# Rope of the second tile half a step sooner, row units between the last transposes, and the first band tile's copies reordered

## The reference

```
x = x + band_attention(layernorm(x), ctx, ctx)     # keys within 128 rows; one head of 512; others weigh exp(-1e9)
y = layernorm(x)                                    # stream of the two layers
for l in (0, 1):
    q, k, v = split(shift_token(y) @ wqkv[l])       # 8 heads of 64
    q, k = l2norm(q) * q_scale, l2norm(k) * k_scale
    q, k = rotary with xpos scale (q, k)            # "rope"
    y = y + local_attention(q, k, v) @ wo[l]        # 256 rows back
    y = y + gated_gelu_ffn(layernorm(shift_token(y)))
x = x + y
```

## Time and profile before

| | us |
|---|---|
| median of 3 runs | 2882.83 (2881.66 to 2883.5) |
| profiled execution, its own time | 2882.62 |
| its span, first to last instruction | 2880.8 |
| PE busy | 2863.6 |
| DVE busy | 2069.0 |
| ACT busy | 1346.0 |
| POOL busy | 1308.8 |

### The profile page before, as it was taken

The page is one execution under the profiler, slowest core; times in us unless marked ns, Lnnn a source line. Parts: engine busy times, 40 slices in busy tenths (PEclk is TensorE's granted clock), DMA queues, the critical chain, the costliest instruction groups (busy, mean ns, idle before and its releaser), DMA issues. The chain is left out here.

```text
span 2880.8 us, 53016 instructions
## 1 busy us (share of the span) xinstructions
PE 2863.6 (99%) x20256; PEld 2521.9 (88%) x20256; DVE 2069.0 (72%) x4135; ACT 1346.0 (47%) x2807; POOL 1308.8 (45%) x1406
## 2 busy tenths in 40 slices
PE   9999999999999999999999999999999999999999
PEld 7887888888889999999998888888888999999998
DVE  8987677776677666766657777776677776676765
ACT  7875556565564222222235566655555322223221
POOL 7857676776641211122105676776662223222221
PEclk9999999999999999999999999999999999999999
DMA  6753233322047777777783223332127777777775
GB/s 218 237 187 109 94 109 103 121 92 81 30 178 299 271 273 265 269 265 258 262 312 120 96 94 108 111 118 90 51 66 294 278 276 272 274 288 281 282 268 195
DMA packets 184897, 547.02 MB, mean 190 GB/s; under 512 B 26678, under 2 KB 82490, under 8 KB 162116
## 3 DMA queue, kind: packets, MB, share of 16 engines
q1 hardware_dynamic: 184500, 543.57, 53.0%
q10 hardware_dynamic: 144, 0.07, 0.0%
HBM read 447.11 MB, written 93.70 MB: 188 GB/s over the span
## 5 line engine op out<-in xcount | busy, mean ns | idle before, releaser
L1251 PE MATMUL quad<-fhT_f,slot_f 128*128 128x256 f32 (+1 forms) x2088 | 594.6, 285 | 0.0
L1252 PE MATMUL quad<-fhT_f,slot_f 128*128 128x256 f32 (+1 forms) x2088 | 590.0, 283 | 0.0
L1253 PE MATMUL quad<-fhT_f,slot_f 128*128 128x256 f32 (+1 forms) x2088 | 589.9, 283 | 0.0
L1253 PEld LDWEIGHTS quad<-fhT_f,slot_f 128*128 128x128 f32 (+1 forms) x2088 | 392.7, 188 | 0.0
L1252 PEld LDWEIGHTS quad<-fhT_f,slot_f 128*128 128x128 f32 (+1 forms) x2088 | 392.7, 188 | 0.0
L1251 PEld LDWEIGHTS quad<-fhT_f,slot_f 128*128 128x128 f32 (+1 forms) x2088 | 392.5, 188 | 0.0
L1674 ACT ACTIVATE gate_f_raw<-gate_f_raw,bias_f 128x512 f32<-128x512 f32 (+1 forms) x176 | 127.2, 723 | 551.1 <-DVE gate_f_raw L2097 551.1
L1542 ACT ACTIVATE lprob<-lprob,small 128x384 f32<-128x384 f32 (+2 forms) x512 | 288.7, 566 | 138.5 <-DVE small L1893 138.5
L2187 POOL TENSOR_SCALAR stats<-stats 128x1 f32<-128x1 f32 x64 | 35.4, 553 | 690.1 <-DVE stats L2037 689.3
L2304 POOL TENSOR_TENSOR turned_qk<-with_cos,with_sin 128x256 f32<-128x256 f32 x252 | 183.1, 747 | 334.3 <-DVE with_sin L1917 242.4
L1000 PE MATMUL bank_pair<-wqkv_h,hT 128*128 128x512 f32 x992 | 323.6, 407 | 0.0
(11 more groups left out here) (296 smaller groups left out, 7469.1 us busy)
## 6 DMA issues: line engine op xcount, KB each, us to landing
slot_f<-parts SPq DMA_DIRECT2D x160, 1792.0 KB, 7.5
slot_f<-parts SPq DMA_DIRECT2D x16, 1190.0 KB, 5.2
s_in<-stream SPq DMA_DIRECT2D x128, 128.0 KB, 2.8
s_res<-stream SPq DMA_DIRECT2D x64, 256.0 KB, 2.9
stream<-a_out SPq DMA_DIRECT2D x64, 256.0 KB, 2.0
res_f<-stream SPq DMA_DIRECT2D x63, 256.0 KB, 7.2
h_in_f<-stream SPq DMA_DIRECT2D x112, 128.0 KB, 6.7
parts<-part_high SPq DMA_DIRECT2D x20, 512.0 KB, 2.6
```

Of the source, the lines that this page charges most:

```text
L1251: e.matmul(bank[0:n, :], high, row_high, start=c == 0, stop=False)
L1252: e.matmul(bank[0:n, :], high, row_low, start=False, stop=False)
L1253: ins = e.matmul(bank[0:n, :], low, row_high, start=False, stop=c == 1)
```

## The change

1. `rotated_tile`: tile 1 is rotated in step 1, in its second half; none in step 2. ACT squares tile 1 in step 1 before `split_q(0)`. DVE does `norm_sum(1)` and the two q ropes before `split_q(0)`, the two k ropes between `split_q(0)` and `split_k(0)`. POOL does all of tile 1's rotation in step 1, ahead of the divisions of tile 0.
2. PE in the second half of steps 2 to 32: in step 2 the transposes of queries and keys now stand ahead of the last six projection matmuls, not behind; in step 31 they stand between three and three; in step 32 `turn_unit` 2 and 3 stand between `turn_q` and `turn_k`.
3. band: ACT's `band_turn_ctx` is cut in two (`band_keep_ctx` has the copy of the value rows); the key copy of tile 0 comes in step 0, ahead of the first query's normalisation. DVE takes the statistics of query tile 3 behind the minimum of tile 0.

```diff
--- before.py
+++ after.py
@@ -481,7 +481,7 @@
 
     def rotated_tile(s):
 
-        return 0 if s == 0 else s - 1 if 2 <= s <= TILES else None
+        return s if s < 2 else s - 1 if 3 <= s <= TILES else None
 
     def rotated_by_gpsimd(l, t, part):
 
@@ -1202,16 +1202,18 @@
                         project_out(tail, 0)
                     if d and ended and s not in (TILES - 1, TILES, TILES + 1):
                         project_out(tail, 1)
+                    ahead = PROJECTED[1][1] + (3 if s == TILES - 1 else 0)
+                    if (s, d) == (TILES - 1, 1):
+                        project(l, s, PROJECTED[1][1], ahead)
+                    if d and 2 <= s <= TILES:
+                        turn_q(s - 1)
                     if (s, d) == (TILES, 1):
                         turn_unit(l, 2)
                         turn_unit(l, 3)
-                    if (s, d) in ((2, 1), (TILES - 1, 1)):
-                        project(l, s, PROJECTED[1][1], PROJECTED[1][2])
                     if d and 2 <= s <= TILES:
-                        turn_q(s - 1)
                         turn_k(s - 1)
-                    if inside and d and s not in (2, TILES - 1):
-                        project(l, s, PROJECTED[1][1], PROJECTED[1][2])
+                    if inside and d:
+                        project(l, s, ahead, PROJECTED[1][2])
                     if mixing:
                         mix(*turned)
                     if (s, d) == (TILES + 2, 0):
@@ -1437,7 +1439,11 @@
             w.wait_ge(S("ctx_turned"), t + 1)
             w.wait_ge(S("mix"), t - TPB + 2)
             copy(B.keyT_h[:, :, k * P:(k + 1) * P], banks[0].rearrange("p (c n) -> p c n", c=KC)).then_inc(S("keyT_high"), 1)
+
+        def band_keep_ctx(t):
+            k = t % TPB
             wait_ctx_rows(w, t)
+            w.wait_ge(S("mix"), t - TPB + 2)
             copy(B.ctx_h[:, k, :], ctx_rows(t)).then_inc(S("ctx_high"), 1)
 
         def normalise(to, source, st):
@@ -1505,8 +1511,10 @@
                     split_h(0, 0)
                 if 0 <= s - 2 < TILES:
                     band_turn_query(s - 2)
+                if 0 < s - 1 < TILES:
+                    band_turn_ctx(s - 1)
                 if 0 <= s - 1 < TILES:
-                    band_turn_ctx(s - 1)
+                    band_keep_ctx(s - 1)
                 if 0 <= s - 6 < TILES:
                     band_put_stream(s - 6)
                 if s == TILES + 4:
@@ -1519,6 +1527,8 @@
                 if s >= TPB:
                     for t in sums_at(s):
                         band_total(t)
+                if s == 0:
+                    band_turn_ctx(0)
                 if s < TILES:
                     band_normalise_query(s)
 
@@ -1586,7 +1596,7 @@
                     turned = (t, 0) if d else (t - 1, 1)
                     if l and (s, d) == (0, 0):
                         split_h(l, 1)
-                    if d == 0 and rotated_tile(s) is not None and (l or s):
+                    if d == (s == 1) and rotated_tile(s) is not None and (l or s):
                         square(l, rotated_tile(s))
                     if d and ended:
                         split_out(tail)
@@ -1834,7 +1844,7 @@
                 if s < TPB:
                     for t in sums_at(s - 1):
                         band_total(t)
-                if s < TILES:
+                if s < TILES and s != 3:
                     band_query_statistics(s)
                 if s >= TPB:
                     for t in sums_at(s - 1):
@@ -1855,6 +1865,8 @@
                     band_turn_ctx(s - 1)
                 if 0 <= s - 3 < TILES:
                     band_exponents(s - 3)
+                if s == 3:
+                    band_query_statistics(s)
                 if 0 <= s - 2 < SUM_AHEAD:
                     band_first_ctx_low(s - 2)
                 for k in first_quarters(s):
@@ -1956,12 +1968,12 @@
                         split_h(1)
                     if l and (s, d) == (0, 0):
                         norm_sum(l, 0)
-                    if (s, d) == (2, 0):
+                    if (s, d) == (1, 1):
                         norm_sum(l, 1)
-                    if d == 0 and rotated_tile(s) is not None:
+                    if d == (s == 1) and rotated_tile(s) is not None:
                         rope(rotated_tile(s), 0, A.with_cos, A.rope_cos, "with_cos")
                         rope(rotated_tile(s), 0, A.with_sin, A.rope_sin, "with_sin")
-                    if d == 0 and rotated_tile(s) and s > 2:
+                    if d == 0 and s > 2 and rotated_tile(s):
                         norm_sum(l, rotated_tile(s))
                     if early is not None:
                         early_centre(l, early)
@@ -1979,7 +1991,7 @@
                     if (s, d) == (TILES + 1, 1):
                         add_first(l, 0, 0)
                         down_split(l, 0)
-                    if d == 0 and rotated_tile(s) is not None:
+                    if d == 0 and s != 1 and rotated_tile(s) is not None:
                         rope(rotated_tile(s), 1, A.with_cos, A.rope_cos, "with_cos")
                         rope(rotated_tile(s), 1, A.with_sin, A.rope_sin, "with_sin")
                     if (s, d) == (0, 0):
@@ -1990,6 +2002,9 @@
                         early_scale(l, early)
                     if d and 1 <= s <= TILES:
                         split_q(s - 1)
+                    if (s, d) == (1, 1):
+                        rope(1, 1, A.with_cos, A.rope_cos, "with_cos")
+                        rope(1, 1, A.with_sin, A.rope_sin, "with_sin")
                     if d == 0 and prepared_item(s, 2) is not None:
                         split_parts(l, prepared_item(s, 2))
                     if d == 0 and prepared_item(s, 1) is not None:
@@ -2327,11 +2342,11 @@
                     sum_parts(prepared_item(s, 1))
                 if summed_rows(s, 1) is not None:
                     sum_first_rows(summed_rows(s, 1))
-                if s == 2:
+                if s == 1:
                     inverse_norm(l, 1)
                 if rotating is not None:
                     rotate(rotating, 0)
-                if rotating and s > 2:
+                if s > 2 and rotating:
                     inverse_norm(l, rotating)
                 if live:
                     divide(t, 1)
```

## The result

| us | before | after |
|---|---|---|
| median | 2882.6 (2881.48 to 2884.64, 12 runs) | 2889.51 (2888.0 to 2891.52, 12 runs) |
| profiled execution, its own time | 2882.62 | 2889.19 |
| its span | 2880.8 | 2887.4 |

The ratio is 1.0024, with a 95% interval of 1.0017 to 1.0031: slower, by more than the 0.2% that a measurement can tell and above the range. The forecast was +1.1 us; measured is +6.9.

A forecast was written before the change was run, and what follows sets the result against it. PE bounds the kernel, busy 2863.6 of 2880.8 us. Layer 0 +1.1, layer 1 +2.2, tail -0.5, band -1.7 give +1.1 us: 2883.7 for the profiled execution, 2884.0 median; range 2879.0 to 2887.0.

The forecast's parts named there:

- Part 1, cost: Step 1: tile 1's work on DVE delays tile 0's first scores, +2.3 us in layer 0, +3.4 us in layer 1.
- rival 2: Step 1: moved ropes cost nothing, first scores not delayed; -4.6 us, 2878.2 us in all; chance 0.10.
- rival 4: Layer 1's new 3.5 us wait lowers TensorE's clock; 2891 us (chance 0.03), or a shorter drop (0.03).
- the short one: Shorter clock drop behind layer 1's new wait: +1.5 to +3 us, 2885.5 to 2887 us; chance 0.03.
- the long form: Low clock from layer 1's first scores for 14 us, work costing half its length again: +7, 2891 us; chance 0.03.
- (b): Step 2, second half: transposes ahead of six projections, less a new 0.5 us wait for ACT's copy; -0.9 us per layer.
- (a): Second half of tile 0's scores: second pair no longer waits for `split_h(3)` behind the ropes; -0.3 us per layer.
- Part 2: Last tiles: step 31's scores lose their key-copy wait, -0.27 us per layer; step 32's reordering worth 0.
- Part 3: Band start: earlier key copy, and statistics behind the minimum remove PE's 1.34 us idle; -1.7 us in all.
- DVE needs only the scores: Band: with statistics behind it, tile 0's minimum waits only for scores and comes near 12.7, transposes ready at 13.8.
- just covered: Band: POOL's two context sums end near 18.1, before PE's total would come at 18.25.
- Rival 3: Band: the gain is lost again to a DMA or POOL's sums; 2885.7 us; chance 0.12.

The follow-up runs named there:

- e3_fill: Changed kernel plus 10 (layer 0) and 15 (layer 1) useless matmuls of 512 columns in PE's waits before the first scores; 2885.7 us, ratio 1.0011.
- e7_band_only: Kernel before with only the band's part of the change; 2881.99 us, ratio 0.9997.
- e1_first: Kernel before with only the first part (tile 1 rotated in step 1, transposes ahead of step 2's last projections); 2889.4 us, ratio 1.0022.
- e2_rest: Changed kernel with its first part undone; band and steps 31 and 32 stay changed; 2880.65 us, ratio 0.9993.
- e6_norm_early: Changed kernel, but tile 1's ropes and rotation back in step 2 and the last `wo` quarter behind `split_k(0)`; 2880.08 us, ratio 0.9991.
- e8_sums_early: e6_norm_early with POOL's sum of context tile 6 taken before its offset for query 3 in the band; 2879.64 us, ratio 0.999.
- Five and nine: Changed kernel with 5 (layer 0) and 9 (layer 1) useless matmuls in the waits before the first scores; 2886.09 us, ratio 1.0012.
- two and five: Changed kernel with 2 (layer 0) and 5 (layer 1) useless matmuls in the waits before the first scores; 2889.57 us, ratio 1.0026.

## Why the prediction was wrong

**Bounds and method.** Right. PE is the bound, every new wait is paid, and start times gave the two new waits to 0.1 us.

**Part 1, cost.** Right. +2.3 and +3.4 were forecast, +2.29 and +3.41 came. The ropes do not come free: rival 2 is out.

**The step that failed: the clock.** The sum took every stretch at full clock, and rival 4 gave a drop behind the layer 1 wait 0.06 in all, 0.03 for the short one. It fell behind both waits: +1.55 and +1.58, 3.1 us, shown by e3_fill. The price of one drop was right for the short form (+1.5 to +3), but I counted only layer 1. The rate of the long form was wrong: at 0.50 a piece of work costs nearly its whole length again (1.28 us for 0.70), not half of it, so 14 us of work would have cost about 12 and not 7. The error was to take "nothing here shows what 3.5 us does" for a low chance; it is a reason for a middling one, and the 2.4 us wait of layer 0 was as far outside the rows of before (1.34 at most) and should have had the same rival. The Trainium skill, "TensorE: Matmul & The Clock Gate", section Why this matters for your kernels, warns of long idle gaps between bursts of matmuls. The trace agrees, with 0.50 behind the wait of 3.49 us; the wait of 2.37 us is shorter than the gaps that the section warns of, and the clock fell behind it too, so there the measurement decides. With both drops as measured the sum is +4.2, 2887.1, at the edge of the range; the band's and (b)'s missing gains below, 1.55 and 0.6, and 0.3 from the FFNs make the +6.6 of this execution.

**Part 1, gain.** (a) right: -0.33 and -0.32 for -0.3. (b) mis-sized: -0.60 each for -0.9. The new wait for ACT's copy was right: 0.35 recorded, 0.6 by starts (the transposes come 0.95 behind those of the probabilities, which need 0.35 of it). But the eight query and key transposes and six projections, then the product, took 237.96 - 234.99 = 2.97, and I had counted 0.72 + 1.5 + 0.55 = 2.77. That is 0.2 of the 0.3 missed, the later start the rest. POOL's divisions stayed covered.

**Part 2.** Right: -0.28 and -0.24 for -0.27 each; the 0.6 us bubble moved from one pair of transposes to the other and stayed.

**Part 3.** The term -1.7 was mis-sized: -0.15 in this execution, -0.55 between the medians of e7_band_only and the kernel before, -1.0 on average over the ten profiles that have it. The step was "DVE needs only the scores". It also needs the second and third query tiles, which land at different times in different executions, and which the wait of 1.61 us used to hide. What I gave as POOL "just covered" was late by 0.15. Rival 3 (0.12), the gain lost again to a DMA, describes this execution; over the ten, somewhat over half of the gain stayed.

**What else moved.** The start of the second FFN is 0.78 us later. DVE waits there for a row block read back from DRAM, 0.24 us before and 1.02 here:

```profile
2198.18 0.69 DVE L2051 BATCH_NORM_STATS2 stats<-h_in_f 128x6 f32<-128x512 f32 x1 [1.02 <-DMA h_in_f<-stream]
```

PE's transposes at 2207.02 wait 0.78 for ACT. The wait is in e1_first too (0.63), with the tail as before, and in e2_rest not in this layer; e6_norm_early has it (0.78) and e8_sums_early, which differs only in the band, has not. So in this layer it goes with the landing more than with the change. It is one of the reasons why single executions differ by 1 us.

## What to carry to other kernels

A new wait of TensorE costs its length and perhaps its clock behind it as well, here some 1.5 us each: in these profiles waits up to 1.34 us and one of 1.91 left it full, 1.44 took it down once in two cases, 2.29 and more each time. Give the second price a real chance for every wait longer than those the trace shows at full clock. Before moving a chain of work earlier, ask which of its instructions the later gain needs; here one reduction and the inverse norm behind it; with the four products and the rotation left where they were, no wait above 0.50 us stood before the first scores and no drop came (e6_norm_early). Taking one DMA wait off a queue shows the next, so its idle time is no gain until the other landings are counted.

## What was not expected of the hardware

- Waits of 2.29 to 3.49 us in a kernel that is otherwise 99% busy lowered the granted clock to 0.50 in every profile that had them, mostly once PE had resumed and once inside the wait, at 1.5 to 2.4 us (7.6 to 8.5 instead of 6.06) a time. There is one profile per kernel; by their mean clock five of the eleven executions with the 2.29 us wait kept full clock. 1.91 us in one place did not lower it, 1.44 in another did. The limit, and what besides length sets it, was not settled.
- Useless matmuls in a wait that cannot be avoided are worth 1.9 us per wait here (e3_fill). Five and nine do most of it, two and five nothing by the median.
